# Unread TensorE products behind the last real one of three stages: 24, 28 and 18 of them

## The reference, cut to what matters

```
x = x + tanh(g_xattn[1]) * _L1_xattn_ref(_layernorm(x), ctx_1024, mask_BxS2_bf1, ...)      # cross attention, 16 heads
x = x + tanh(g_ffn[1]) * _L1_ffn_ref(_layernorm(x), gate_W, w1_e, w3_e, w2_e, ...)         # mixture: 8 experts, 2 a token, and shared ones
x = x + tanh(g_xattn[2]) * _L2_xattn_ref(_layernorm(x), ctx_1024, ctx_1024, ...)           # local attention, windows of 64
x = x + tanh(g_ffn[2]) * _L2_ffn_ref(_layernorm(x), w_gate, w_up, w_down)                  # feed-forward on integers
x = x + tanh(g_xattn[3]) * _L3_xattn_ref(_layernorm(x), ctx_1024)                          # a scan over the tokens
```

## Time and profile before

| | us |
|---|---|
| median of 3 runs (2026.86 to 2030.92) | 2026.98 |
| the profiled execution's own time | 2035.54 |
| its span, first to last instruction | 2033.5 |
| TensorE busy in it (91%) | 1859.5 |
| VectorE busy (62%) | 1259.9 |
| ScalarE busy (41%) | 828.6 |
| GpSimd busy (14%) | 275.1 |

### The profile page before, as it was taken

How to read it: one execution, slowest core, us unless ns; L and a number is a source line. 1 busy time by engine, 2 the same in 40 slices (tenths; PEclk the granted TensorE clock), 3 DMA queues, 4 the chain that set the end, 5 groups by cost and what they waited for, 6 DMA issues and landing times. The chain is left out here.

```text
span 2033.5 us, 38758 instructions
## 1 busy us (share of the span) xinstructions
PE 1859.5 (91%) x13655; PEld 1505.6 (74%) x13680; DVE 1259.9 (62%) x4621; ACT 828.6 (41%) x2246; POOL 275.1 (14%) x498
## 2 busy tenths in 40 slices
PE   8899998999998998999999998997992989999978
PEld 6567766677666997999999998776551877777745
DVE  7768875877785261111111135677788539999988
ACT  3433435655564111111111111775486424444468
POOL 2001112000001061000000045432000320000032
PEclk9999998999999899999999999899995989999989
DMA  6211112121111812222222011110100031111100
GB/s 229 89 55 47 47 47 78 43 84 42 43 42 28 282 63 99 85 85 88 88 85 85 26 50 56 58 44 9 61 1 0 0 107 35 36 38 40 23 11 32
DMA packets 106723, 124.96 MB, mean 61 GB/s; under 512 B 36160, under 2 KB 85832, under 8 KB 104776
## 3 DMA queue, kind: packets, MB, share of 16 engines
q1 hardware_dynamic: 95704, 107.64, 15.9%
q0 software_dynamic: 3072, 8.39, 1.3%
q10 hardware_dynamic: 7792, 6.95, 1.0%
HBM read 86.39 MB, written 36.63 MB: 60 GB/s over the span
## 5 line engine op out<-in xcount | busy, mean ns | idle before, releaser
L1804 DVE TENSOR_TENSOR me_h<-me_sg,me_ps_u 128x512 f32<-128x512 f32 x106 | 72.8, 686 | 279.2 <-PE me_ps_u L1615 262.7
L1756 ACT ACTIVATE me_sg<-me_ps_g 128x512 f32<-128x512 f32 x106 | 63.3, 597 | 371.8 <-PE me_ps_g L1615 337.9
L1276 ACT ACTIVATE ca_e<-ca_scored,ca_neg_max 128x256 f32<-128x256 f32 x256 | 127.3, 499 | 110.2 <-DVE ca_neg_max L1335 110.2
L1615 PE MATMUL me_ps_g<-me_x_turned,me_w 128*128 128x128 f32 x1184 | 144.3, 275 | 1.9 <-issue 1.9
L1615 PE MATMUL me_ps_u<-me_x_turned,me_w 128*128 128x128 f32 x1184 | 144.3, 275 | 0.0
L1615 PEld LDWEIGHTS me_ps_g<-me_x_turned,me_w 128*128 128x128 f32 x1184 | 140.7, 192 | 4.3 <-issue 2.1
L1623 PE MATMUL me_ps_y<-me_w,me_h 128*128 128x256 f32 x592 | 140.0, 379 | 0.0
L1615 PEld LDWEIGHTS me_ps_u<-me_x_turned,me_w 128*128 128x128 f32 x1184 | 138.2, 192 | 0.0
L2964 ACT ACTIVATE sc_y_all<-ss_v 128x16 f32<-128x16 f32 x256 | 60.9, 238 | 156.1 <-DVE ss_v L3027 156.1
L1623 PEld LDWEIGHTS me_ps_y<-me_w,me_h 128*128 128x128 f32 x592 | 106.8, 190 | 11.4
L1335 DVE CUSTOM_DVE_ANT_0 ca_scored<-ca_main,ca_mask_add 128x256 f32<-128x256 f32 x256 | 92.9, 419 | 26.0 <-PE ca_main L1219 26.0
(11 more groups left out here) (451 smaller groups left out, 4332.2 us busy)
## 6 DMA issues: line engine op xcount, KB each, us to landing
me_w<-in_L_ffn_w_e SPq DMA_DIRECT2D x24, 1024.0 KB, 8.4
ca_k_list<-kv_out SPq DMA_DIRECT2D x28, 256.0 KB, 2.3
ca_v_list<-kv_out SPq DMA_DIRECT2D x28, 256.0 KB, 2.3
sk_gb<-scan_g_band SPq DMA_DIRECT2D x14, 512.0 KB, 3.7
moe_x_list<-me_zeros SPq DMA_DIRECT2D x1, 5248.0 KB, 21.1
me_x_tile<-moe_x_list SPq DMA_DIRECT2D x38, 128.0 KB, 2.0
moe_y_list<-me_y ACTq DMA_DIRECT2D x37, 128.0 KB, 1.7
ca_kT<-ca_k_list SPq DMA_DIRECT2D x4, 1024.0 KB, 4.8
```

Of the source, the lines that this page charges most:

```text
L1276: nc.scalar.activation(e[:, g % 3, e_, it, :], scored[:, g % 2, e_, it, :], ACT.Exp, scale=-1.0, bias=neg_max[:, g % 2, n:n + 1], accum_ou ...
L1615: last = nc.tensor.matmul(ps[:, j * P:(j + 1) * P], w[:, n, kt, f:f + P], x[:, kt, :], start=(kt == 0), stop=(kt == KD - 1))
L1756: nc.scalar.activation(sg[:, c, :], ps_g[c][:, :], ACT.Silu).then_inc(done, 1)
L1804: nc.vector.tensor_tensor(h[:, c, :, :].rearrange("p j n -> p (j n)"), sg[:, c, :], ps_u[c][:, :], ALU.mult).then_inc(done[c], 1)
```

## The change

Behind the last real product of each of three stages, TensorE gets unread products: 24 behind cross attention, 28 behind the mixture, 18 behind the integer feed-forward. Each is 128x128 by 128x128 in float32, of the identity with itself, into a PSUM tile that nothing reads any more in that stage. No wait and no semaphore is added.

```
@@ stage_cross_attention
+    SEAM = 24
@@ block.tensor
             walk(scores, fill, turn, weigh)
+            for _ in range(SEAM):
+                nc.tensor.matmul(ps_av[0][:, 0:P], core.ident[:, :], core.ident[:, :], start=True, stop=True)
@@ stage_moe
+    SEAM = 28
@@ block.tensor
             for i in range(LATE):
                 late(i)
+            for _ in range(SEAM):
+                nc.tensor.matmul(ps_r[:, 0:P], core.ident[:, :], core.ident[:, :], start=True, stop=True)
@@ int_gate_first
+    SEAM = 18
@@ block.tensor
             schedule(pe, TILES, ((2, turn_h), (3, down)))
+            for _ in range(SEAM):
+                nc.tensor.matmul(idle[:, 0:P], core.ident[:, :], core.ident[:, :], start=True, stop=True)
```

## The result

The changed kernel takes 2035.20 us (median of 7 runs, 2034.09 to 2038.71), the kernel before in the same session 2028.81 us (7 runs, 2026.35 to 2030.92). The ratio is 1.0039, with a 95% interval of 1.0030 to 1.0048, or 7.9 us (6.1 to 9.7). Taken once more in another session (`after_again`) it was 1.0035 (1.0021 to 1.0048), or 7.1 us. The change makes the kernel slower, as forecast, but by 1.0 to 1.8 us more than the 6.1 us of the forecast.

What follows compares the result with a forecast made beforehand. VectorE was taken to set all three stage ends, TensorE having 2.65, 3.66 and 2.62 us of slack. (2.75 - 0.55) + 2.6 + (1.4 - 0.1) = 6.1 us on 2026.98 gave 2033.1 us; range 2026.5 to 2036.5.

Steps and rivals of the forecast that it cites:

- barriers that wait and little given back: At the three stage ends: next stages start later by 6.75 us in all, little regained; chance 0.54.
- the term of the scan products: Scan products at the full clock: TensorE through 3.3 us earlier, but a SyncE chain ends together; gain 0.1 us.
- displaced code: Rival: added products shift TensorE's code, moving a hole; up to 3 us either way, most likely 0; chance 0.08 on top.
- Slack and barrier: At the three ends: products exceed TensorE's slack and the drain waits, delaying next stages by 2.75, 2.6 and 1.4 us.
- The rival without waiting: At the three ends: barriers do not wait for the products; no change, 2027.4 us; chance 0.20.
- The price of a product: Unread products at the ends: two records each, 0.112 to 0.118 us a record at the full clock.
- Transposes of the mixture: Mixture's start: transposes at the full clock, paced by ScalarE's copies, end about 5.4 us in, not 6.0; gain 0.55 us.
- Logits: Mixture's logits: clock falls again in gapless work, so gain taken as 0; bound 3.3 us.
- Local attention: Local attention's start: first 8.85 us gain nothing, clock falls again during the fill; gain 0, bound 2.4 us.
- The sum: Whole kernel: delays at the three ends less gains in the stages behind them, 6.1 us slower.

Runs made afterwards that it cites:

- after_again: The changed kernel, unedited, profiled and timed once more in another session, against the kernel before: ratio 1.0035.
- Fit: Products at the three ends cut from 24, 28 and 18 to 10, 15 and 10; ratio 1.0049 against the kernel before.
- tiny: The changed kernel's 24, 28 and 18 products with 32 x 64 operands in place of 128 x 128; ratio 0.9998 against the kernel before.
- ig_only: Only the 18 products behind the integer feed-forward, the 24 and 28 of the changed kernel removed; ratio 1.0013 against the kernel before.
- the second pair: Unedited kernel before and changed kernel, each profiled once more in the same session: spans of 2036.8 and 2044.5 us.

## Why the prediction was off, and what of it held

**The step that failed.** The mechanism held, barriers that wait and little given back; two terms did not. In the sum it is the term of the scan products, where I had TensorE "through 3.3 us earlier" and a gain of 0.1: it was 0.5 to 0.6 us earlier, and the stage grew by 0.4 us in both pairs (36.1 to 36.5, 36.3 to 36.7), which is no gain, though small beside the spread of its length. Beside the sum it is displaced code, put at "up to 3 us either way, most likely 0" from rows that have nothing to do with it: it costs 8 to 11 us of local attention in four kernels with other counts, and shows as 1.1 to 1.5 us of waits in this one. What share of the 1.0 to 1.8 us between forecast and result each of the two has stays open. The details are below.

**Slack and barrier, right.** The drain waits for the products. Forecast delays 2.75, 2.6 and 1.4; measured 2.68, 2.57 and 1.36, and again within 0.02 in after_again. Fit and tiny show the other half: with the products over before VectorE, the seams cost nothing. The rival without waiting is refuted.

**The price of a product, right.** 0.112 to 0.118 us a record; measured (6.41 - 0.286) / 55 = 0.111 at the mixture's seam. The 0.19 to 0.20 that I read for the low clock comes from a stretch whose clock was mixed (0.59 over the 5.53 us of `WARM`), and no term used it.

**Transposes of the mixture, right.** The copies are through at 659.19 (start 658.05, 1.14 long), 5.3 us into the stage in place of 6.0: 0.7 against 0.55.

**Logits, right.** The clock fell again at 663, in the middle of gapless work. The 64 records took 10.36 us in place of 10.45, so nothing was given back.

**Local attention, right in the main.** The clock fell 3.5 us into the stage, and the first exponents came at 1269.38, 8.84 us into it. The low stretch ended sooner than before, 13.5 us into the stage and not 19, and the stage was 0.8 to 1.3 us shorter. ig_only, with no products ahead of the stage, has the same 153.7 us, so I do not credit this to the change.

**Scan products, off.** I wrote that TensorE would be through 3.3 us sooner. Its last group started 1641.39 - 1621.40 = 19.99 us into the stage in place of 1648.24 - 1627.64 = 20.60: 0.6 us. It ran into a wait that the low clock had hidden, 1.66 us for ScalarE's `sp_xT`, ScalarE itself being held by the transfer of `scan_g`. SyncE's wait at the end did not grow by 3 us either (1.0 after 1.6; 1.7 and 1.7 in the second pair). Forecast was a gain of 0.1 us, measured a loss of 0.4, and that too lies within the spread of this stage, 36.1 to 38.0 us without the seam.

**The sum, 6.1 against 7.1 and 7.9.** The terms now read 2.68 + 2.57 + 1.36 - 0.7 + 0.4 = 6.3, 0.8 and 1.6 us short. The intervals of both ratios hold 6.3, and the stages of single executions cannot place the rest: the integer feed-forward is +2.1 us in the pair where the seam gives 1.4, but its length spreads by 1.4 without any seam; the mixture is +3.5 where 2.57 - 0.7 gives 1.9, with a thin stretch of varying length in it. One candidate is the displaced code of the changed kernel itself, 1.1 and 1.5 us of such waits (next paragraph), which would bring the sum to 7.4 and 7.8; but local attention is no longer for them, 153.8 us against 153.7 in ig_only, and so that stays open.

**Displaced code, a true mechanism and mis-sized.** I priced it at up to 3 us, from the earlier trace rows, which was the wrong evidence: that stretch does not move with the code. The true one is the block boundary, worth 8 to 11 us of local attention, and which kernel pays it hangs on the number of instructions ahead. With 52 products ahead TensorE loses 0.7 us at `la_av` (1.1 in after_again) and 0.4 at `la_turned` to such waits; had the stage had 24, 25 or 28 ahead, the change would have cost some 9 us more. That the forecast came as near as it did is in this respect luck.

## What to carry to other kernels

An engine with slack before a stage's end has exactly that slack for unread work, and pays for the rest in full: size it by its measured record time, 10, 15 and 10 products here. A stage with runs of very short products can change a whole kernel by 0.4 to 0.5% when any instruction of TensorE is added ahead of it; before a small change is judged, look whether an untouched stage has changed its length and has waits put down to issue, and repeat the edit with as many instructions that cost no time. One profile is one execution: here the first pair, an 8 us hole in one of them, said that the slower kernel was the faster.

## What the hardware showed that I had not expected

- TensorE stopped for up to 2.2 us at a boundary of its 16 KB code blocks that falls late into a run of products 14 ns apart, in up to 7 places of a stage, 767 to 769 recorded instructions (three blocks) apart, and once 1,024 (four). It went on 1.2 to 1.6 us after a block had come.
- Most boundaries show no such stop, and among them are some as late in a fast run, whose block had come 2.3 us or more before.
- Four kernels with 96 to 112 instructions more ahead of local attention wait there for 8.8 to 11.5 us at `la_av` in all; those with 208 for 0.7 to 1.1 us; those with 0 and 256 have no such row, and the one with 216 has none at `la_av` and 1.1 us at `la_turned`.
- A thin stretch of some 7 us in the mixture is there in some executions of the same code and not in others.
